# Moving three steps of ScalarE's queue ahead of the first two evictions of a tile, in gated attention with feed-forward on 8 cores

## The chip, the cores and the metric

The kernel runs on one Trainium2 chip, on all 8 of its cores (two dies of four). Each core takes one of 8 sequences of 4096 tokens and talks to no other core. The time is the device time in microseconds of the slowest core.

## What is computed

A layer of gated attention with a residual and a layer norm, and then a feed-forward network with a residual and a layer norm. Cut to what matters here:

```python
normed = (x - mu) * rsqrt(var + 1e-05) * norm_g + norm_b
hv = silu(normed @ W_h + b_h)              # 1024 -> 4096
v, gate = hv[..., :2048], hv[..., 2048:]
qk = silu(normed @ W_qk + b_qk)            # 1024 -> 128
quad_q, lin_q, quad_k, lin_k = four scaled and shifted copies of qk
attn = square(relu(quad_q @ quad_k.T / 256 + rel_bias))   # in groups of 256 tokens
lin_kv = lin_k.T @ v / n                   # over the whole sequence
out = (gate * (attn @ v + lin_q @ lin_kv)) @ W_o + b_o + x
x = layernorm(x + out)
x = layernorm(x + relu(x @ W1 + b1) @ W2 + b2)
```

## The kernel before

Everything is written out by hand, one queue of instructions per engine, with semaphores between them. `NT` is 32: the 4096 tokens of a core are 32 tiles of 128. There are three phases. Phase 1 makes v, gate and the four heads of each tile, writes them to HBM and adds up lin_kv. Phase 2 does the attention, W_o and the first layer norm. Phase 3 is the feed-forward network. Phase 2 begins only when phase 1 has ended, since it needs the whole lin_kv. Only phase 1 is touched by the change.

PSUM is held as two tensors of four banks: E0 and E1. In phase 1 banks 0 and 1 of E0 take the 512-wide outputs of the big product in turn, banks 2 and 3 of E0 take the transposed tile, and E1 takes qk (its first 128 columns), the transposed lin_k and the product for lin_kv.

PE's order in tile t (`emit_tensor`, from L653) is: `p1_T(t+1)` (L592, L598: eight 128-wide transposes of the next tile's normed input), `p1_hv(t,0)` and `p1_hv(t,1)` (a bias matmul on L623 and eight 512-wide matmuls on L626 each), `p1_qk(t+1)` (L610: eight 128-wide matmuls that read the next tile's `nfm`), `p1_hv(t,2)`, `p1_hv(t,3)`, `p1_linkT(t)` (L635), `p1_hv(t,4)`, `p1_hv(t,5)`, `p1_linkv(t)` (L645), `p1_hv(t,6)`, `p1_hv(t,7)`. Slices s = 0 to 3 are v, 4 to 7 are gate. An even slice waits until both slices of the pair ahead of it have been evicted, since a pair takes both banks:

```python
if s % 2 == 0:
    wge(tn, "c_hvev", 8 * t + s)       # L619
```

`p1_qk(u)` waits for both halves of `nfm` of tile u (`c_Tev`, L607) and for DVE's addition of lin_kv of tile u-2 (L608).

ScalarE (ACT) evicts and, for each tile, runs these helpers in the order of the loop from L887. `p1_hvev(t,s)` is a Silu from PSUM into `vt` (L865) or `gt` (L872). `p1_ev(t+1)` is two copies of the transposed next tile from PSUM into `nfm` (L845, L847). `p1_n0(t+2)` normalizes the tile after that (L835). `stats_sq(t+8)` is a square with a sum (L821), and in every fourth tile (t = 3, 7, ... 23, six in all) `sqrt_batch` follows it, a square root that waits for six small DVE instructions and needs another function table (L827). `p1_qkev(t+1)` is the Silu of qk into `qkf` (L854). It waits for p1_qk(t+1) on PE (`c_qk`) and for DVE's heads of tile t-1.

DVE, in tile t, takes the sums of tile t+8, then makes the four heads from `qkf` (L1150 to L1157), copies lin_k (L1161) and adds to lin_kv (L1167). SyncE loads x ten tiles ahead and stores v. ACT's own queue stores the gate (`g_sp`), and GpSimd stores the heads and casts W1 and W2 to bf16 in HBM, two pieces a tile.

Of the kernel before, what the change touches and what calls it, by code (L numbers as in the profile page):

```python
# [61 lines left out]
def build_program(NT=32, dbg=False, phases=3):  # L62
# [223 lines left out]
    def wge(eng, nm, v):  # L286
        if v > 0:
            eng.wait_ge(S[nm], v)
# [520 lines left out]
    def emit_scalar(sc):  # L809
# [8 lines left out]
        def stats_sq(u):  # L818
            D["x1"].wait(sc, u)
            wge(sc, "c_sqst", u - 1)  # L820
            sc.activation(T["sqscr"][:, (u % 2) * DM:(u % 2 + 1) * DM],  # L821
                          T["xt"][:, (u % XB) * DM:(u % XB + 1) * DM],
                          AF.Square, accum_out=T["sumsq"][:, u:u + 1]).then_inc(S["c_sqst"], 1)

        def sqrt_batch(g):
            wge(sc, "c_v1", g + 1)
            sc.activation(T["s_all"][:, 4 * g:4 * g + 4], T["rcp"][:, 4 * g:4 * g + 4],  # L827
                          AF.Sqrt).then_inc(S["c_sq1"], 1)

        def p1_n0(u):  # L830
            if not (0 <= u < NT):
                return
            wge(sc, "c_sv", u // 4 + 1)
            wge(sc, "c_T", 2 * u - 4)
            sc.activation(T["n0"][:, (u % 3) * DM:(u % 3 + 1) * DM],  # L835
                          T["xt"][:, (u % XB) * DM:(u % XB + 1) * DM],
                          AF.Identity, bias=T["nms"][:, u:u + 1],
                          scale=T["s_all"][:, u:u + 1]).then_inc(S["c_n0"], 1)

        def p1_ev(u):  # L840
            if not (0 <= u < NT):
                return
            wge(sc, "c_T", 2 * u + 1)
            wge(sc, "c_hvmm", 8 * u - 8)
            sc.copy(T["nfm"][:, (u % 2) * DM:(u % 2) * DM + 512], E0[:, 1024:1536]).then_inc(S["c_Tev"], 1)  # L845
            wge(sc, "c_T", 2 * u + 2)
            sc.copy(T["nfm"][:, (u % 2) * DM + 512:(u % 2) * DM + 1024], E0[:, 1536:2048]).then_inc(S["c_Tev"], 1)  # L847

        def p1_qkev(u):
            if not (0 <= u < NT):  # L850
                return
            wge(sc, "c_qk", u + 1)
            wge(sc, "c_heads", u - 1)
            sc.activation(T["qkf"][:, (u % 2) * QKD:(u % 2 + 1) * QKD],  # L854
                          E1[:, 0:QKD], AF.Silu,
                          bias=T["bqk_eff"][:]).then_inc(S["c_qkev"], 1)

        def p1_hvev(t, s):
            wge(sc, "c_hvmm", 8 * t + s + 1)
            src_ = E0[:, (s % 2) * 512:(s % 2) * 512 + 512]  # L860
            if s < 4:
                if s == 0:
                    D["vout"].wait(sc, t - 2)
                    wge(sc, "c_lkvmm", t - 1)
                sc.activation(T["vt"][:, (t % 2) * HID + s * 512:(t % 2) * HID + (s + 1) * 512],  # L865
                              src_, AF.Silu).then_inc(S["c_hvev"], 1)
            else:
                h = (s - 4) // 2
                if s in (4, 6):
                    D["gout"].wait(sc, 2 * (t - 2) + h)  # L870
                gslot = ((t % 2) * 2 + h) * DM
                sc.activation(T["gt"][:, gslot + (s % 2) * 512:gslot + (s % 2) * 512 + 512],  # L872
                              src_, AF.Silu).then_inc(S["c_hvev"], 1)
                if s in (5, 7):
                    wge(sc, "c_hvev", 8 * t + s + 1)
                    D["gout"].issue(sc, g_sp[t * 128:(t + 1) * 128, h * DM:(h + 1) * DM],
                                    T["gt"][:, gslot:gslot + DM])
# [7 lines left out]
        p1_ev(0)  # L885
        p1_qkev(0)
        for t in range(NT):  # L887
            p1_hvev(t, 0)
            p1_hvev(t, 1)
            p1_ev(t + 1)  # L890
            p1_n0(t + 2)
            u = t + L
            if u < NT:
                stats_sq(u)
                if u % 4 == 3:
                    sqrt_batch(u // 4)
            p1_hvev(t, 2)
            p1_hvev(t, 3)
            p1_qkev(t + 1)
            p1_hvev(t, 4)  # L900
            p1_hvev(t, 5)
            p1_hvev(t, 6)
            p1_hvev(t, 7)
# [87 lines left out]
        for Ti in range(NS):  # L991
# [7 lines left out]
            for tt in range(4):  # L999
                t = 4 * Ti + tt  # L1000
# [265 lines left out]
    with nc.Block() as block:  # L1266
        @block.vector
        def _(ve):
            emit_vector(ve)

        @block.sync
        def _(sync):
            emit_sync(sync)

        @block.gpsimd
        def _(gp):
            emit_gpsimd(gp)

        @block.tensor
        def _(tn):  # L1280
            emit_tensor(tn)

        @block.scalar
        def _(sc):
            emit_scalar(sc)
# [35 lines left out]
```

## Time and profile before

| | us |
|---|---|
| median of 3 runs | 2492.0 |
| lowest and highest | 2488.97, 2530.39 |
| the profiled execution | 2487.91 |
| its longest span, core 3 | 2486.4 |
| its shortest span, core 5 | 2467.1 |
| core 3: PE busy, weight loads busy | 2031.6, 860.0 |
| core 3: DVE, ACT, GpSimd busy | 541.4, 729.5, 96.7 |

A span runs from the first to the last instruction of a core. PE is TensorE's matmuls, PEld its weight loads, which lie beside them. A row of the timeline merges instructions of one kind; its bracket tells how long the engine stood idle before it and what ended the idle time. Ends of matmuls are modelled, so a PE row overlaps the next by a little. PEclk is the clock that TensorE was granted, as a share of its full 2.4 GHz.

### The profile page before, as it was taken

To read this page: it belongs to the slowest core of one execution; us is meant where nothing else is said; L and a number is where in the kernel's file an instruction comes from. 1 tells how busy PE (TensorE), PEld (TensorE's weight loads), DVE (VectorE), ACT (ScalarE), POOL (GpSimd) and SP (SyncE) were. 2 spreads that over 40 slices of the span, in tenths; PEclk is the share of its full clock that TensorE was granted. 3 is DMA by queue.
4 is the path that set the end of the run, shared out by engine and by line. 5 is a ranking of instruction groups with operands and counts; after the bars stand their busy time and mean duration, and the time that the engine had idled before them with its cause. 6 is when DMAs were issued, how large, how long until landed. Compare 5 with 4: busy or idle time off the path is not lost.

```text
span 2486.4 us, 27942 instructions; the slowest of 8 cores (2467.1 to 2486.4 us)
## 1 busy us (share of the span) xinstructions
PE 2031.6 (82%) x9498; PEld 860.0 (35%) x9498; DVE 541.4 (22%) x1127; ACT 729.5 (29%) x1192; POOL 96.7 (4%) x177
## 2 busy tenths in 40 slices
PE   0348888888888864888888858989898989898988
PEld 0113333333333321333333423434343434343433
DVE  0331221212211112444444420202020202020202
ACT  0034333333332311333333323132323232323231
POOL 1001101100111000000000000000000000000000
PEclk9869999999999987999999979999999999999999
DMA  9454433443433248766656634202020102020101
GB/s 142 69 141 102 128 114 97 133 114 105 115 90 102 87 119 247 200 195 186 192 190 193 191 89 142 74 15 72 16 70 18 67 13 73 14 78 11 51 17 51
DMA packets 125173, 256.28 MB, mean 103 GB/s; under 512 B 57614, under 2 KB 66119, under 8 KB 122985
## 3 DMA queue, kind: packets, MB, share of 16 engines
q1 hardware_dynamic: 80794, 129.42, 16.6%
q10 hardware_dynamic: 27648, 92.29, 11.5%
q0 software_dynamic: 16592, 32.78, 8.5%
q8 instruction: 80, 1.31, 0.2%
q14 instruction: 59, 0.48, 0.1%
HBM read 188.64 MB, written 112.20 MB: 121 GB/s over the span
## 4 chain that ended last, share of the span: by engine, by line
PE 72%; ACT 7%; DVE 6%; issue 6%; DMA 3%; another core or an unknown queue 3%; SPq 1%; DVEq 1%; ACTq 0%
PE E L626 19%; PE E L787 18%; PE E L770 16%; PE E L738 10%; PE E L623 3%; ACT h L996 2%; DVE sums L1218 1%; PE E L645 1%; PE E L717 1%; DMA xt<-x 1%; PE E L733 1%; DMA w<-w1bf_sp 1%; ACT vt L865 1%; DVE pre L1214 1%
## 5 line engine op out<-in xcount | busy, mean ns | idle before, releaser
L626 PE MATMUL E<-wh,nfm 128*128 128x512 bf16 x2048 | 524.0, 402 | 0.0
L770 PE MATMUL E<-xfm,w 128*128 128x512 bf16 x2048 | 457.1, 382 | 73.6 <-ACT h L996 59.4
L787 PE MATMUL E<-w,h 128*128 128x512 bf16 x2048 | 453.2, 379 | 0.0
L770 PEld LDWEIGHTS E<-xfm,w 128*128 128x128 bf16 x2048 | 197.5, 98 | 331.8 <-issue 106.1
L626 PEld LDWEIGHTS E<-wh,nfm 128*128 128x128 bf16 x2048 | 187.1, 102 | 265.8 <-issue 100.7
L787 PEld LDWEIGHTS E<-w,h 128*128 128x128 bf16 x2048 | 195.1, 98 | 241.2 <-issue 14.6
L996 ACT ACTIVATE h<-E,b_fm 128x512 bf16<-128x512 f32 x256 | 173.5, 686 | 315.4 <-PE E L770 315.4
L738 PE MATMUL E<-wo,gfm 128*128 128x512 bf16 x1024 | 253.8, 405 | 0.0
L1251 DVE TENSOR_TENSOR pre<-E,x2r 128x1024 f32<-128x1024 f32 x32 | 39.2, 1225 | 860.8 <-PE E L787 860.8
L872 ACT ACTIVATE gt<-E 128x512 f32<-128x512 f32 x128 | 76.5, 597 | 248.1 <-PE E L626 245.4
L738 PEld LDWEIGHTS E<-wo,gfm 128*128 128x128 bf16 x1024 | 100.3, 103 | 139.3 <-issue 46.0
L865 ACT ACTIVATE vt<-E 128x512 bf16<-128x512 f32 x128 | 75.8, 597 | 233.5 <-PE E L626 220.7
L1003 ACT ACTIVATE sq<-pre 128x1024 bf16<-128x1024 f32 x32 | 33.8, 1057 | 367.9 <-DVE pre L1251 367.9
L623 PE MATMUL E<-bh_eff_bf,ones 1*128 1x512 bf16 x256 | 101.1, 395 | 42.2 <-ACT vt L865 29.3
L1167 DVE TENSOR_TENSOR linkv<-linkv,E 128x2048 f32<-128x2048 f32 x31 | 70.9, 2288 | 180.5 <-PE E L645 180.5
L717 PE MATMUL E<-ident,gtm 128*128 128x128 bf16 x512 | 46.9, 228 | 74.0 <-ACT gfm L936 62.0
L699 PE MATMUL E<-v,attnT 128*128 128x512 bf16 x256 | 78.8, 390 | 31.6 <-DMA v<-v_sp 30.1
L944 ACT ACTIVATE sq<-pre 128x1024 bf16<-128x1024 f32 x32 | 33.8, 1057 | 206.5 <-DVE pre L1214 182.1
L1161 DVE CAST lktm<-E 128x128 bf16<-128x128 f32 x32 | 9.3, 292 | 351.2 <-PE E L635 351.2
L1197 DVE TENSOR_TENSOR gtm<-E,g 128x512 bf16<-128x512 f32 x128 | 79.3, 681 | 8.4 <-DMA g<-g_sp 8.4
L936 ACT CAST gfm<-E 128x512 bf16<-128x512 f32 x128 | 69.4, 585 | 8.7 <-PE E L717 5.0
L623 PEld LDWEIGHTS E<-bh_eff_bf,ones 1*128 1x128 bf16 x256 | 23.4, 91 | 137.2 <-issue 134.0
(110 smaller groups left out, 1150.5 us busy)
## 6 DMA issues: line engine op xcount, KB each, us to landing
g_sp<-gt ACTq DMA_DIRECT2D x64, 512.0 KB, 3.6
g<-g_sp ACTq DMA_DIRECT2D x64, 512.0 KB, 6.1
xt<-x SPq DMA_DIRECT2D x32, 512.0 KB, 4.5
v_sp<-vt SPq DMA_DIRECT2D x32, 512.0 KB, 2.9
v<-v_sp SPq DMA_DIRECT2D x32, 512.0 KB, 5.6
x2t<-x SPq DMA_DIRECT2D x32, 512.0 KB, 4.2
x_sp<-x2f ACTq DMA_DIRECT2D x32, 512.0 KB, 5.7
x2r<-x_sp SPq DMA_DIRECT2D x32, 512.0 KB, 4.2
```

The costliest lines, as they stand in the source:

```text
L623: tn.matmul(pslc, T["ones1"][:], T["bh_eff_bf"][0:1, s * 512:(s + 1) * 512], start=True, stop=False)
L626: mm = tn.matmul(pslc, T["nfm"][:, sl2 + c * 128:sl2 + (c + 1) * 128], T["wh"][:, c * 2 * HID + s * 512:c * 2 * HID + (s + 1) * 512], star ...
L699: tn.matmul(ps, T["attnT"][:, a0:a0 + 128], T["v2"][:, (vtile % 3) * HID + b * 512:(vtile % 3) * HID + (b + 1) * 512], start=(j == 0), sto ...
L717: mm = tn.matmul(E0[:, bank + k * 128:bank + (k + 1) * 128], T["gtm"][:, (u % 2) * HID + ch * 128:(u % 2) * HID + (ch + 1) * 128], ID, sta ...
L738: mm = tn.matmul(ps, T["gfm"][:, (u % 2) * HID + k * 128:(u % 2) * HID + (k + 1) * 128], T["wo"][:, k * DM + h * 512:k * DM + (h + 1) * 51 ...
L770: mm = tn.matmul(ps, T["w1"][:, dc * 4096 + ci * 128:dc * 4096 + (ci + 1) * 128], T["xfm3"][:, (Ti % 2) * 4 * DM + dc * 512:(Ti % 2) * 4 * ...
L787: mm = tn.matmul(ps, T["h1"][:, ci * 512 + tt * 128:ci * 512 + (tt + 1) * 128], T["w2"][:, ci * DM + h * 512:ci * DM + (h + 1) * 512], sta ...
L865: sc.activation(T["vt"][:, (t % 2) * HID + s * 512:(t % 2) * HID + (s + 1) * 512], src_, AF.Silu).then_inc(S["c_hvev"], 1)
L872: sc.activation(T["gt"][:, gslot + (s % 2) * 512:gslot + (s % 2) * 512 + 512], src_, AF.Silu).then_inc(S["c_hvev"], 1)
L996: sc.activation(T["h1"][:, ci * 512:(ci + 1) * 512], E0[:, (ci % 4) * 512:(ci % 4 + 1) * 512], AF.Relu, bias=T["b1_fm"][:, ci:ci + 1]).the ...
L1167: ve.tensor_tensor(T["linkv"][:], T["linkv"][:], E1[:, :], ALU.add).then_inc(S["c_lkvadd"], 1)
L1197: ve.tensor_tensor(T["gtm"][:, (tau % 2) * HID + b * 512:(tau % 2) * HID + (b + 1) * 512], E1[:, b * 512:(b + 1) * 512], T["g2"][:, gsl:gs ...
```

## The change

In ACT's loop over tiles, the eviction of the next tile's transposes, the normalization of the tile after it and the eviction of the next tile's qk now stand ahead of the evictions of slices 0 and 1, in the order ev, n0, qkev. The queues of the other engines and all waits inside the helpers stay as they are.

```diff
--- before.py
+++ after.py
@@ -885,10 +885,11 @@
         p1_ev(0)
         p1_qkev(0)
         for t in range(NT):
+            p1_ev(t + 1)
+            p1_n0(t + 2)
+            p1_qkev(t + 1)
             p1_hvev(t, 0)
             p1_hvev(t, 1)
-            p1_ev(t + 1)
-            p1_n0(t + 2)
             u = t + L
             if u < NT:
                 stats_sq(u)
@@ -896,7 +897,6 @@
                     sqrt_batch(u // 4)
             p1_hvev(t, 2)
             p1_hvev(t, 3)
-            p1_qkev(t + 1)
             p1_hvev(t, 4)
             p1_hvev(t, 5)
             p1_hvev(t, 6)
```

## Rows read from the trace of the kernel before

**Rows 1.** The page of the slowest core: chain that ended last, shares by engine.
```profile
PE 72%; ACT 7%; DVE 6%; issue 6%; DMA 3%; another core or an unknown queue 3%; SPq 1%; DVEq 1%; ACTq 0%
```

**Rows 2.** Stage 157.5 to 918 us of core 3: busy by engine, PEclk, DMA share, GB/s.
```profile
157.50:918.00 760.50, 657.49 (x2952) 256.31 (x2951) 152.61 (x258) 266.27 (x447) 85.42 (x160) 0.94 0.39 107
```

**Rows 3.** Waits of PE in that stage: us in total, times, longest us.
```profile
PE E L610 <- ACT nfm L847: 59.3, 31, 1.9
```

**Rows 4.** PE timeline, one tile: start us, us, line, [idle before <-releaser].
```profile
403.79 0.61 PE L610 MATMUL E<-nfm,wqk 128*128 128x128 bf16 x8 [1.92 <-ACT nfm L847]
404.33 0.48 PE L623 MATMUL E<-bh_eff_bf,ones 1*128 1x512 bf16 x1
404.75 3.44 PE L626 MATMUL E<-wh,nfm 128*128 128x512 bf16 x8
...
408.44 1.90 PE L626 MATMUL E<-wh,nfm 128*128 128x512 bf16 x8
410.18 0.22 PE L635 MATMUL E<-ident,lkfm 128*128 128x128 bf16 x1
411.18 0.37 PE L623 MATMUL E<-bh_eff_bf,ones 1*128 1x512 bf16 x1 [0.78 <-ACT vt L865]
...
421.57 0.37 PE L623 MATMUL E<-bh_eff_bf,ones 1*128 1x512 bf16 x1 [0.39 <-ACT gt L872]
```

**Rows 5.** ACT timeline of the same tile.
```profile
402.94 0.60 ACT L847 CAST nfm<-E 128x512 bf16<-128x512 f32 x1
403.41 1.26 ACT L835 ACTIVATE n<-xt,nms,s_all 128x1024 bf16<-128x1024 f32 x1
404.56 1.06 ACT L821 ACTIVATE sqscr<-xt 128x1024 bf16<-128x1024 f32 x1
...
410.44 0.60 ACT L865 ACTIVATE vt<-E 128x512 bf16<-128x512 f32 x1 [1.55 <-PE E L626]
410.93 0.36 ACT L854 ACTIVATE qkf<-E,bqk_eff 128x128 f32<-128x128 f32 x1
```

**Rows 6.** Granted clock (third value from the right) in 404.6 to 407.9 us.
```profile
404.60:407.90 3.30, 3.30 (x9) 1.05 (x8) 0.00 (x0) 1.11 (x3) 0.00 (x0) 0.50 0.41 84
```

**Rows 7.** PE timeline, starts of L610 in three later tiles of core 3.
```profile
427.84 0.61 PE L610 MATMUL E<-nfm,wqk 128*128 128x128 bf16 x8 [1.92 <-ACT nfm L847]
...
452.31 0.61 PE L610 MATMUL E<-nfm,wqk 128*128 128x128 bf16 x8 [1.92 <-ACT nfm L847]
...
453.16 1.90 PE L626 MATMUL E<-wh,nfm 128*128 128x512 bf16 x8
...
474.71 0.61 PE L610 MATMUL E<-nfm,wqk 128*128 128x128 bf16 x8 [1.92 <-ACT nfm L847]
```

**Rows 8.** ACT timeline of the tile at 426 us, which loads two tables.
```profile
431.61 1.28 ACT L827 ACT_TABLE_LOAD   x1 [1.85 <-DVE rcp L1117]
...
434.42 1.08 ACT L865 ACTIVATE vt<-E 128x512 bf16<-128x512 f32 x2
```

**Rows 9.** PE timeline of two tiles with table loads, core 3, then core 1.
```profile
722.73 0.37 PE L623 MATMUL E<-bh_eff_bf,ones 1*128 1x512 bf16 x1 [1.58 <-ACT vt L865]
...
332.60 0.58 PE L623 MATMUL E<-bh_eff_bf,ones 1*128 1x512 bf16 x1 [2.28 <-ACT vt L865]
333.12 3.59 PE L626 MATMUL E<-wh,nfm 128*128 128x512 bf16 x8
```

**Rows 10.** PE timeline of core 3, the first of the tiles.
```profile
163.98 0.61 PE L610 MATMUL E<-nfm,wqk 128*128 128x128 bf16 x8 [1.80 <-ACT nfm L847]
```

**Rows 11.** Lines L626 and L770 on core 1, then the same on core 3.
```profile
L626 PE MATMUL E<-wh,nfm x2048: 379/379/634, 155.2 to 907.1; 128*128 128x512 bf16 x187
...
L770 PE MATMUL E<-xfm,w x2048: 376/379/634, 1468.5 to 2401.9; 128*128 128x512 bf16 x187
...
L626 PE MATMUL E<-wh,nfm x2048: 379/379/634, 157.6 to 916.1; 128*128 128x512 bf16 x187
...
L770 PE MATMUL E<-xfm,w x2048: 376/379/634, 1483.7 to 2416.7; 128*128 128x512 bf16 x187
```

## What the change should do to the time

> **What bounds the kernel now.** I read the chain that ended last first, and PE holds 72% of it [rows 1]. So an edit counts if it shortens PE's stalls, or makes its matmuls faster, in the stage where it is made. That stage is phase 1, from 157.5 to 918 us on core 3 [rows 2]. PE is busy there for 657.5 of 760.5 us, its clock is 0.94, and ACT is busy for only 266.3 us and DVE for 152.6 us. No engine other than PE is full, and the DMA share is 0.39. The other engines matter through the moments at which PE waits for them. In PE's waits the largest stands at L610, p1_qk(t+1), for ACT's second copy into nfm: 59.3 us in 31 waits [rows 3].
>
> One tile shows why. The pair of slices 0 and 1 ends at 401.87 (403.79 less the idle 1.92), and then p1_qk waits 1.92 us [rows 4]. ACT has to evict slice 1 first, because it stands ahead of the two copies in its queue, though the transposes that these copies read ended some 4 us before. The reader is to see a second cost in the same rows: the eight matmuls of L626 after the stall took 3.44 us, those after them 1.90 us. The clock was 0.50, the 1.2 GHz level, from 404.6 to 407.9 us [rows 6], after PE had stood idle for 1.92 us. It is not so in every tile: after the stall that ended at 452.31 the eight took 1.90 us [rows 7]. So from one L610 to the next a plain tile takes 24.05 us with such a fall (403.79 to 427.84) and 22.40 us without (452.31 to 474.71). A fall costs 1.65 us [rows 4, 7]. On core 3 the clock fell after 25 of the 31 stalls, the first of them at 163.98 after only 1.80 us [rows 10]; on the other cores after 14 to 26.
>
> **The change, part by part.** Nothing is added or removed. It moves five ACT instructions: two copies, the normalization and the Silu of qk ahead of Silus of slices 0 and 1. ACT issues no DMA in between, and SP's and POOL's queues are not touched. SP's load of x waits for the normalization, which now comes earlier, but the store of v that stands behind evictions 0 to 3 in SP's order still sets its pace, so nothing starts much sooner.
>
> *The copies and the normalization.* They now follow the last gate eviction and its store, and need the transposes, which are over before slice 0 starts at 421.57 [rows 4]. Two copies of at most 0.60 and the normalization, pitch 1.15 (403.41 to 404.56) [rows 5], are 2.4 us. They lie beside slices 0 and 1, which take 4.35 us (421.57 to 425.92, which is 427.84 less 1.92) [rows 4, 7]. Cost nothing, with near 2 us of cover. So p1_qk no longer waits: a stall of 1.92 us goes.
>
> *What is late next.* The Silu of qk is a new wait in front of the evictions of slices 0 and 1, which before ran under slice 1 and under the stall. Slice 2 needs both banks free, so PE waits behind p1_qk instead, for three ACT instructions. After the pair ends, p1_qk ends 0.45 us later: it starts 0.16 before the modelled end, as L635 does (408.44 + 1.90 = 410.34, L635 at 410.18), and its row is 0.61 long [rows 4]. ACT starts 0.10 later, as at 410.44 after 410.34. Then comes the Silu of qk, 0.36 long [rows 5]. No row shows an eviction directly behind it. Neighbours on ACT overlap by 0.11: 0.60 long and 0.49 apart, 1.26 long and 1.15 apart [rows 5]. I take 0.25; without overlap it would be 0.36, and below 0.25 nothing points. The two evictions are 0.49 and 0.60, and PE starts 0.14 after them (410.44 + 0.60 to 411.18) [rows 4, 5]. So the new stall is 0.10 + 0.25 + 0.49 + 0.60 + 0.14 = 1.58 us (up to 1.69), and slice 2 starts 0.45 + 1.58 = 2.03 us after the pair's end. Before, it was 404.33 less 401.87, 2.46 us [rows 4]. A tile gains 0.43 us (0.32 to 0.43).
>
> The Trainium skill, "ScalarE: Activation LUTs", section "What ACT_TABLE_LOAD costs", says that back-to-back ACTIVATEs overlap by about 93 ns. By that the pitch would be 0.27 and the stall 1.60 us, the sum hardly other.
>
> *The clock.* This is the larger term. After stalls between 1.06 and 1.62 us no fall follows anywhere in phase 1, on any core, some 30 in all; one is the 1.58 at 722.73 [rows 9]. After 1.80 it fell [rows 10], after 1.92 mostly. The new stall is nearest to 722.73, so I take no fall in a plain tile. The bounds are none and all 31. What speaks against it is that small matmuls (p1_qk) now stand ahead of the stall and not behind.
>
> *Tiles with table loads.* In six tiles the square is followed by DVE's small instructions (a wait of 1.85), a table load, the root, and a second load, before the evictions of slices 2 and 3 at 434.42 [rows 8]. This chain, not PE, sets when slice 4 starts, with or without a fall at slice 2. It begins with the square, 2.69 us after the pair's end (404.56 less 401.87) [rows 4, 5]. In the new order that is 0.45 + 0.10 + 0.25 + 0.49 + 0.49 = 1.78, so slice 4 starts 0.91 us earlier. PE reaches it earlier too: slice 3 ends 2.03 + 4.35 = 6.38 after the pair, and slice 4 starts at 434.42 + 1.08 + 0.14 less 425.92 less 0.91, 8.81. The stall there is some 2.4 us. The nearest row is core 1's 2.28, behind which L626 took 3.59 [rows 9]. Over the eight cores ten of sixteen such stalls were followed by a fall. I take three of six at 1.65 each, 5.0 us. The bounds are none and six falls that reach over both slices, 6 x 3.3 = 19.8 us.
>
> *Downstream.* From the last L626 to the first L770 core 3 took 567.6 us, while core 1, which was 9 us ahead, took 561.4 [rows 11]. Until now the cores came out of phase 1 apart, since they had different numbers of falls; with none they come out together and load W1 together. I leave core 3's own 567.6 and add 3 us for the slowest of eight with different luck in the table tiles; the bounds are 0 and 6.
>
> **The sum**, on core 3, the slowest, against the profiled 2487.9 us: 25 plain tiles x 0.43 = 10.8. Nineteen of these had a fall, 19 x 1.65 = 31.4. Six table tiles x 0.91 = 5.5. Together 47.7. Less 5.0 and less 3 leaves 39.7 us, so 2448 us. The median of the runs before, 2492.0, is 4 us above the profiled one, and the lowest is 2489.0; I take the lower end and stay at 2448.
>
> **Rivals.**
>
> *1. The forecast*: no falls in plain tiles, about half in table tiles. 2448 us, its own range 2441 to 2458. Chance 0.57.
>
> *2. Falls almost gone from phase 1.* The new stalls in table tiles mostly miss, or the cores' loads at the start of phase 2 collide less. Without the 5.0 and the 3 it is 2487.9 - 47.7 = 2440, and with core 1's passage (6 us less) 2434. The only thing for it is that six of sixteen such stalls were not followed by a fall [rows 9]. Chance 0.17.
>
> *3. The fall moves with the stall.* 1.58 to 1.69 us lies just under the 1.80 that was followed by one [rows 10]. If 19 plain tiles still have it, only 10.8 + 5.5 - 5.0 = 11.3 us remain: 2477 us. Against it speaks the 1.58 of core 3 [rows 9]. Chance 0.17. The Trainium skill, "TensorE: Matmul & The Clock Gate", section "A second HAM failure mode: psum-queue depth-cycling", says that short idles between groups of matmuls as banks are cycled are enough to make the clock oscillate. By that rule the new stall would do what the old one did. The trace shows it for the 1.92 us stall and does not for those of 0.78 us.
>
> *4. The other side: a fall after each of the 31 new stalls, and a double one in each table tile.* Core 3 had 25 falls. In plain tiles there would be six more, 6 x 1.65 = 9.9 against the 10.8 gained. In table tiles 19.8 are lost against 5.5. That gives 2487.9 - 10.8 + 9.9 - 5.5 + 19.8 = 2501 us. It turns slower than before once falls in phase 1 cost more than 16.3 us above those of before, ten more than now. It needs all 31 stalls to be hit, where the longer ones of today are missed 6 times in 31. Chance 0.06.
>
> *5. A plain delay on ACT*, such as extra table loads from the new order, 2 x 1.28 us a tile [rows 8], 79 us over 31 tiles. Today the Silu of slice 3 is followed by the Silu of qk and copies by the normalization with no load between [rows 5], and the order brings no new pair of functions but those. Chance 0.03.
>
> **How the numbers follow.** The likeliest is 2448 us. From 2436 to 2478 lie rivals 1 and 3 and most of 2, a bit over 8 in 10. A measurement of this kernel can tell about 2% from no change. Faster by over 2% is under 2438 us: half of rival 2 and a tail of the forecast, 0.18. Slower by over 2% is over 2538 us: rival 5, 0.03. Within 2%: 0.79.
>
> **What would show it.** L610 has no idle time behind nfm any more. The idle time stands at L623 of slice 2, released by ACT's vt, 1.6 us in 25 plain tiles. L626 of slice 2 is 1.90 long and not 3.3 to 3.4; a plain tile takes 21.97 us. Slice 4 of a table tile waits 2.4 us. PEclk of phase 1 rises from 0.94 to 0.98 or more, and the stage is some 43 us shorter, while phases 2 and 3 keep their length. It would be wrong if slice 2 shows over 1.75 us of idle time, if L626 behind it still takes 3.4, or if copies or normalization outlast slice 1.

## The result: 0.7% faster, where 1.6% was forecast

| | before | after |
|---|---|---|
| median of 10 runs | 2490.1 us | 2474.3 us |
| lowest | 2487.5 us | 2465.9 us |
| the profiled execution | 2487.9 us | 2465.9 us |
| its longest span | 2486.4 us (core 3) | 2464.4 us (core 5) |

The ratio of after to before is 0.9928, with a 95% interval from 0.9915 to 0.9941. In some executions the cores of one die run at a lower clock; the ratio leaves these out. By this ratio the kernel is faster beyond doubt, by 18 us, and by less than 2%. The forecast was 2448 us, 40 us faster. The measured 2474.3 lies inside the range, 2436 to 2478, but where rival 3 put it (2477) and not where the likeliest case did.

The stalls moved as the prediction had it. These are PE's waits in phase 1 of core 5, the slowest (us in total, times, longest us):

```profile
PE E L623 <- ACT vt L865: 81.9, 64, 2.3
PE E L623 <- ACT gt L872: 12.8, 32, 0.8
```

The wait at L610 for nfm [rows 3] is gone. In its place L623 waits for vt 64 times and not 33.

In PE's timeline three tiles of core 5 follow each other here (start, us, line, idle before):

```profile
433.92 0.61 PE L610 MATMUL E<-nfm,wqk 128*128 128x128 bf16 x8
436.17 0.37 PE L623 MATMUL E<-bh_eff_bf,ones 1*128 1x512 bf16 x1 [1.64 <-ACT vt L865]
436.47 1.90 PE L626 MATMUL E<-wh,nfm 128*128 128x512 bf16 x8
...
455.93 0.61 PE L610 MATMUL E<-nfm,wqk 128*128 128x128 bf16 x8
458.18 0.37 PE L623 MATMUL E<-bh_eff_bf,ones 1*128 1x512 bf16 x1 [1.64 <-ACT vt L865]
458.48 3.27 PE L626 MATMUL E<-wh,nfm 128*128 128x512 bf16 x8
...
479.54 0.61 PE L610 MATMUL E<-nfm,wqk 128*128 128x128 bf16 x8
```

p1_qk starts with no idle time, and slice 2 then waits 1.64 us. From one L610 to the next it is 22.01 us from 433.92 (forecast 21.97) and 23.61 us from 455.93. In the first of these tiles L626 behind the stall is 1.90 long, in the second 3.27. The stall is 1.64 us in both. The granted clock (third value from the right) behind the first stall and behind the second is:

```profile
436.50:438.40 1.90, 1.90 (x10) 0.76 (x9) 0.00 (x0) 0.56 (x2) 0.00 (x0) 1.00 1.44 164
459.00:462.20 3.20, 3.20 (x8) 0.84 (x6) 0.00 (x0) 0.43 (x2) 0.00 (x0) 0.50 0.90 108
```

ACT's timeline of another tile:

```profile
385.05 0.59 ACT L847 CAST nfm<-E 128x512 bf16<-128x512 f32 x1
385.52 1.25 ACT L835 ACTIVATE n<-xt,nms,s_all 128x1024 bf16<-128x1024 f32 x1
389.05 0.37 ACT L854 ACTIVATE qkf<-E,bqk_eff 128x128 f32<-128x128 f32 x1 [2.28 <-PE E L610]
389.32 1.07 ACT L865 ACTIVATE vt<-E 128x512 bf16<-128x512 f32 x2
390.27 1.07 ACT L821 ACTIVATE sqscr<-xt 128x1024 bf16<-128x1024 f32 x1
```

The copies and the normalization are over at 386.8, well ahead of the Silu of qk at 389.05. That Silu and the next eviction start 0.27 apart, where the estimate was 0.25. Of a tile with table loads:

```profile
416.85 0.22 PE L635 MATMUL E<-ident,lkfm 128*128 128x128 bf16 x1
419.34 0.37 PE L623 MATMUL E<-bh_eff_bf,ones 1*128 1x512 bf16 x1 [2.27 <-ACT vt L865]
419.64 1.90 PE L626 MATMUL E<-wh,nfm 128*128 128x512 bf16 x8
```

Slice 4 waits 2.27 us, where 2.4 was forecast. And the whole of phase 1 on core 5 (busy us by engine, then the granted clock, the DMA share and GB/s):

```profile
core 5: us, PE busy (x) PEld busy (x) DVE busy (x) ACT busy (x) POOL busy (x), PEclk, DMA share, GB/s
151.00:887.00 736.00, 640.86 (x2952) 255.11 (x2951) 152.59 (x258) 266.12 (x447) 85.41 (x160) 0.96 0.47 110
```

It is 735 us long where core 3 took 759 before. Its clock is 0.96, against 0.94 [rows 2] and the 0.98 or more that the forecast wanted to see. Over the eight cores the clock fell after 116 of 240 stalls of 1.58 to 1.64 us, nearly all of them 1.64 (13 to 16 of 30 on each core). Before the change it fell after 149 of 240 stalls of 1.92 us.

### The profile page after: what moved, and what is told of

Read it like the earlier page. It is cut to its first block, busy times and chain, and to the rows that moved or that the text cites. A ratio compares the mean times of both kernels' runs of the same rounds, so it can differ in the third digit from the quotient of the medians.

```text
span 2464.4 us, 27942 instructions; the slowest of 8 cores (2452.0 to 2464.4 us)
## 1 busy us (share of the span) xinstructions
PE 2019.7 (82%) x9498; PEld 860.5 (35%) x9498; DVE 541.4 (22%) x1127; ACT 728.8 (30%) x1192; POOL 96.7 (4%) x177
## 4 chain that ended last, share of the span: by engine, by line
PE 73%; ACT 7%; DVE 6%; issue 6%; DMA 3%; another core or an unknown queue 3%; SPq 1%; DVEq 1%; ACTq 0%
PE E L626 19%; PE E L787 18%; PE E L770 17%; PE E L738 10%; PE E L623 3%; ACT h L996 2%; ACT vt L865 2%; DVE sums L1218 1%; PE E L645 1%; PE E L717 1%; DMA xt<-x 1%; DMA w<-w1bf_sp 1%; PE E L733 1%; DVE pre L1214 1%
## 5 line engine op out<-in xcount | busy, mean ns | idle before, releaser
L770 PE MATMUL E<-xfm,w 128*128 128x512 bf16 x2048 | 461.5, 384 | 74.9 <-ACT h L996 59.3
L626 PE MATMUL E<-wh,nfm 128*128 128x512 bf16 x2048 | 510.4, 394 | 0.0
L770 PEld LDWEIGHTS E<-xfm,w 128*128 128x128 bf16 x2048 | 198.6, 99 | 336.5 <-issue 113.5
L626 PEld LDWEIGHTS E<-wh,nfm 128*128 128x128 bf16 x2048 | 183.8, 100 | 256.9 <-issue 85.3
L623 PE MATMUL E<-bh_eff_bf,ones 1*128 1x512 bf16 x256 | 100.4, 392 | 94.7 <-ACT vt L865 81.9
L623 PEld LDWEIGHTS E<-bh_eff_bf,ones 1*128 1x128 bf16 x256 | 23.4, 91 | 189.2 <-issue 189.2
```

Of the source, the lines that this page charges most:

```text
L623: tn.matmul(pslc, T["ones1"][:], T["bh_eff_bf"][0:1, s * 512:(s + 1) * 512], start=True, stop=False)
L626: mm = tn.matmul(pslc, T["nfm"][:, sl2 + c * 128:sl2 + (c + 1) * 128], T["wh"][:, c * 2 * HID + s * 512:c * 2 * HID + (s + 1) * 512], star ...
L770: mm = tn.matmul(ps, T["w1"][:, dc * 4096 + ci * 128:dc * 4096 + (ci + 1) * 128], T["xfm3"][:, (Ti % 2) * 4 * DM + dc * 512:(Ti % 2) * 4 * ...
```

## The experiments

Two theories of these falls were put against each other. **A**: the eight 128-wide matmuls of p1_qk, which stand directly at the stall, are part of what brings the clock down. **B**: a stall of 1.64 us does it by its length alone, whatever stands beside it, and the quiet stalls of this length before the change [rows 9] were a few lucky ones. A third, **C**, sought the lost gain at the start of phase 2.

The falls below are counted from the clock records of all eight cores, for the stalls of one kind in phase 1. A stall counts as followed by a fall when a stretch at the lower clock begins during it or within about 2 us of its end.

### e2_small_away and e3_small_ahead: the same stall, with and without small matmuls directly ahead

Both lengthen the stall in the same way, by scratch copies on ACT ahead of eviction 1. Both have p1_qkev behind eviction 3 again. Only e2 moves p1_qk on PE.

```diff
@@ e2_small_away, against the changed kernel @@
 (PE)
             p1_hv(t, 0)
-            p1_hv(t, 1)
             p1_qk(t + 1)
+            p1_hv(t, 1)
             p1_hv(t, 2)
 (ACT)
             p1_ev(t + 1)
             p1_n0(t + 2)
-            p1_qkev(t + 1)
             p1_hvev(t, 0)
+            p1_dummy(t)
             p1_hvev(t, 1)
...
             p1_hvev(t, 3)
+            p1_qkev(t + 1)
@@ the new helper on ACT @@
+            wge(sc, "c_hvmm", 8 * t + 2)
+            for w in (256, 256):
+                wge(sc, "c_dmy", ndmy[0])
+                sc.copy(T["dmy"][:, 0:w], E0[:, 512:512 + w]).then_inc(S["c_dmy"], 1)
+                ndmy[0] += 1
@@ e3_small_ahead: the same on ACT with (256, 256, 256), PE as in the changed kernel @@
```

> As e1, but PE runs p1_qk(t+1) between slices 0 and 1, so that a full slice stands ahead of the stall, and ACT makes two copies of 256 columns of bank 1 into a scratch tile ahead of eviction 1, which stretch the stall at slice 2 to about 1.64 us. Tile length 22.0 us without a fall, as in the changed kernel. Theory A: no falls in plain tiles, phase 1 of about 714 us and a time near 2448. Theory B: falls after about half of the stalls, phase 1 of 735 and a time near 2472, as in the changed kernel.

> The control of e2: the same scratch copies on ACT, three of them, but p1_qk(t+1) stays directly ahead of the stall, which is again about 1.64 us. Both theories: falls after about half of the stalls and a time near 2472. If it had no falls, neither the small matmuls nor the stall's length would be the cause, but something in the order of ACT's work.

e2 took 2463.1 us, ratio 0.9882 (0.9858 to 0.9905). e3 took 2480.2 us, ratio 0.9941 (0.9912 to 0.9969). PE's timeline of one tile of e2 (p1_qk is L611 here, the slices L624 and L627), and under it all of phase 1 on the same core, with columns as above:

```profile
389.39 0.61 PE L611 MATMUL E<-nfm,wqk 128*128 128x128 bf16 x8
389.94 0.38 PE L624 MATMUL E<-bh_eff_bf,ones 1*128 1x512 bf16 x1
390.25 1.90 PE L627 MATMUL E<-wh,nfm 128*128 128x512 bf16 x8
393.78 0.37 PE L624 MATMUL E<-bh_eff_bf,ones 1*128 1x512 bf16 x1 [1.62 <-ACT vt L866]
394.08 1.90 PE L627 MATMUL E<-wh,nfm 128*128 128x512 bf16 x8
...
161.00:880.00 719.00, 621.95 (x2952) 251.99 (x2951) 152.51 (x258) 285.91 (x508) 85.36 (x160) 0.99 0.39 113
```

PE's timeline of e3, the stall of a tile with a fall and of the next without, and then phase 1:

```profile
380.90 0.37 PE L624 MATMUL E<-bh_eff_bf,ones 1*128 1x512 bf16 x1 [1.64 <-ACT vt L866]
381.20 2.67 PE L627 MATMUL E<-wh,nfm 128*128 128x512 bf16 x8
...
402.26 0.61 PE L611 MATMUL E<-nfm,wqk 128*128 128x128 bf16 x8
404.51 0.37 PE L624 MATMUL E<-bh_eff_bf,ones 1*128 1x512 bf16 x1 [1.64 <-ACT vt L866]
404.81 1.90 PE L627 MATMUL E<-wh,nfm 128*128 128x512 bf16 x8
...
163.00:900.00 737.00, 642.43 (x2952) 255.50 (x2951) 152.52 (x258) 297.75 (x539) 85.46 (x160) 0.96 0.40 110
```

The stalls are 1.62 and 1.64 us. In e2 a full slice stands ahead of the stall and p1_qk one slice earlier, in e3 p1_qk stands directly ahead. In e2 the clock fell after none of 230 stalls of 1.62 us or a little less, nor after ten of 1.84. Each core also had one of 1.90 us, and after four of these eight it fell. In e3 it fell after 109 of 240, much like the changed kernel. A plain tile without a fall is 22.0 us in both. e2's granted clock in phase 1 is 0.99, e3's 0.96, and phase 1 is 719 us against 737. This is theory A, and against B: the same idle time, in a tile of the same length, brings the clock down only with the small matmuls directly ahead of it. So the changed kernel's falls come from what the change put next to the stall.

The time of e2 was 15 us above its expectation. 5 us of this lie in phase 1, where 29 of 48 table tiles took 25.2 us or more. The rest is behind phase 1: on its slowest core 577 us from the end of the slices to phase 3's first matmul (L770 before, L771 here), where core 3 took 567 before [rows 11], and 1007.4 us from there to the end, where core 3 took 1002.7. e3 was 8 us above its expectation.

### e8_longer_stall: how much do the small matmuls count?

```diff
@@ against e2_small_away @@
-            for w in (256, 256):
+            for w in (256, 256, 256):
```

> The kernel of e2 with one more scratch copy on ACT ahead of eviction 1: the stall at slice 2, with a full slice ahead of it and behind it, grows from 1.62 to 2.08 us, which is e3's stall of 1.63 plus the 0.45 us that the small matmuls took there. If the small matmuls count for the clock as almost nothing, falls follow after about as many stalls as in e3 (109 of 240). If they count for about half, after clearly more. If a long stall between full slices never brings the clock down, after none. Tile of 22.46 us without a fall; with falls after half of them a time near 2490, without near 2478.

```profile
405.80 1.90 PE L627 MATMUL E<-wh,nfm 128*128 128x512 bf16 x8
409.79 0.45 PE L624 MATMUL E<-bh_eff_bf,ones 1*128 1x512 bf16 x1 [2.08 <-ACT vt L866]
410.17 3.46 PE L627 MATMUL E<-wh,nfm 128*128 128x512 bf16 x8
```

One run took 2506.5 us beside 2495.3 for the kernel before, where 2490 was expected with falls after half of the stalls. The stall is 2.08 us between full slices, and the clock fell after 192 of 222 of them, behind this one too (L627, 3.46). So idle time alone is enough when it is long, and 0.46 us more of it did more than the small matmuls do in e3: they are not the same as idle time. How much less they are is not settled by this run, since the tile is 0.45 us longer too, and e5 shows that the share of falls hangs on more than the stall and its neighbours.

### e1_ev_first: only the copies and the normalization go ahead

```diff
@@ against the changed kernel @@
             p1_ev(t + 1)
             p1_n0(t + 2)
-            p1_qkev(t + 1)
             p1_hvev(t, 0)
...
             p1_hvev(t, 3)
+            p1_qkev(t + 1)
             p1_hvev(t, 4)
```

> Only the two copies and the normalization go ahead of evictions 0 and 1; the Silu of qk stays behind eviction 3. Theory A (the clock falls because the eight small matmuls of L610 stand directly at the stall and count for little): slice 2 waits 0.10 + 0.60 + 0.14 less 0.45 = 0.4 us for eviction 1, and no fall follows in a plain tile. Theory B (the length of the stall alone decides, and 1.64 us is enough): the same, since 0.4 us is short. Both expect a plain tile of 22.40 - 2.46 + 0.85 = 20.8 us (22.0 in the changed kernel), table tiles of 22.4, and about 2410 us against 2488 before. Theory C (the gain is lost again where phase 2 begins, because the cores come out together): a passage from the last L626 to the first L770 longer than 570 us and a time over 2420.

```profile
401.71 0.61 PE L610 MATMUL E<-nfm,wqk 128*128 128x128 bf16 x8
402.71 0.37 PE L623 MATMUL E<-bh_eff_bf,ones 1*128 1x512 bf16 x1 [0.39 <-ACT vt L865]
403.02 1.90 PE L626 MATMUL E<-wh,nfm 128*128 128x512 bf16 x8
...
162.00:841.00 679.00, 618.65 (x2951) 251.47 (x2951) 152.57 (x258) 265.72 (x446) 85.36 (x160) 0.99 0.42 120
```

It took 2419.4 us, ratio 0.9721 (0.9629 to 0.9813), 9 us above its expectation. Slice 2 waits 0.39 us and no fall follows, on any core. A plain tile is 20.77 us. Only in table tiles, whose slice 4 still waits 2.27 us, the clock fell, in 17 of 48. So two of the three steps moved are worth some 50 us more than all three (ratios 0.9721 and 0.9928): the third, the Silu of qk ahead of evictions 0 and 1, costs 1.25 us of stall in each tile and all the falls of plain tiles. Theory C finds something, but little. The passage to phase 3 took 563 to 572 us on the eight cores, before 558 to 567, and three of them passed the 570 us that the theory wanted.

### e4: each slice waits for its own bank

```diff
@@ against e1_ev_first @@
-            if s % 2 == 0:
-                wge(tn, "c_hvev", 8 * t + s)
+            wge(tn, "c_hvev", 8 * t + s - 1)
```

> As e1, and each slice waits for the eviction of its own bank alone (slice s for eviction s-1 and not for both of the pair ahead). The stalls at slices 0, 2 and 4 go (0.39, 0.4 and 0.78 us). Plain tile 19.25 us, no falls; table tiles keep a stall of some 2.35 us at slice 4 and take 21.6 us. 25 x 3.15 + 31 + 6 x 2.9 - 5 = 122 us less than before: about 2366 us. If something other than PE becomes the bound (ACT's chain, the load of x), a plain tile is longer than 19.6 us.

> The kernel of e4 again, for a profile of all eight cores at the granted clock of the other runs. Cores 0 to 3 of e4 took 623 us for phase 1 and 2342 to 2354 us in all; so 2358 us, with no falls in plain tiles, and a plain tile of 19.25 us.

The first gave a ratio of 0.9477 (0.943 to 0.9525). The second took 2359.0 us, ratio 0.9463 (0.9436 to 0.9489), 7 us under the first expectation and 1 us above the second. PE's timeline of the second:

```profile
387.22 0.37 PE L622 MATMUL E<-bh_eff_bf,ones 1*128 1x512 bf16 x1 [1.79 <-ACT vt L864]
...
401.32 0.61 PE L610 MATMUL E<-nfm,wqk 128*128 128x128 bf16 x8
401.86 0.38 PE L622 MATMUL E<-bh_eff_bf,ones 1*128 1x512 bf16 x1
402.18 1.90 PE L625 MATMUL E<-wh,nfm 128*128 128x512 bf16 x8
...
406.07 0.22 PE L634 MATMUL E<-ident,lkfm 128*128 128x128 bf16 x1
406.22 0.39 PE L622 MATMUL E<-bh_eff_bf,ones 1*128 1x512 bf16 x1
```

No slice of a plain tile waits for anything any more, behind p1_qk at 401.32 neither. A plain tile takes 19.01 us, a table tile 21.4 without a fall. This version beats both kernels, by 5.4% and 4.7%.

### e5_own_bank_only and e6_after_own_bank: the own-bank wait with the two other orders

```diff
@@ e5: the kernel before, and e6: the changed kernel @@
-            if s % 2 == 0:
-                wge(tn, "c_hvev", 8 * t + s)
+            wge(tn, "c_hvev", 8 * t + s - 1)
```

> The order of evictions of the kernel before, and each slice waits for the eviction of its own bank alone. The stalls of 0.39 and 0.78 us go, that of 1.92 us at p1_qk stays, since it waits for the copies and these stand behind eviction 1. Theory A: the small matmuls still follow that stall at once, so falls stay as frequent as before (14 to 26 a core); a plain tile takes 21.2 us without and 22.9 with a fall, and the time is 31 x 1.17 = 36 us less than before, about 2453. If the own-bank wait were all that matters, it would be near e4's 2358.

> The changed kernel with own-bank waits. Slice 2 now waits for the Silu of qk and for eviction 0, not for eviction 1: a stall of 0.10 + 0.25 + 0.60 + 0.14 = 1.1 us directly behind the small matmuls. Theory A: at 1.1 us the small matmuls do not bring the clock down (in the changed kernel they did at 1.64), so no falls and a plain tile of 20.35 us, 34 us above e4: about 2392. If the clock still falls after half of them, some 25 us more, 2417.

e5 took 2438.3 us, ratio 0.9819 (0.9742 to 0.9896), e6 2404.3 us, ratio 0.9654 (0.9623 to 0.9684). PE's timelines, e5 and then e6:

```profile
405.24 0.61 PE L610 MATMUL E<-nfm,wqk 128*128 128x128 bf16 x8 [1.92 <-ACT nfm L846]
...
406.10 2.86 PE L625 MATMUL E<-wh,nfm 128*128 128x512 bf16 x8
```

```profile
391.21 0.61 PE L610 MATMUL E<-nfm,wqk 128*128 128x128 bf16 x8
392.98 0.37 PE L622 MATMUL E<-bh_eff_bf,ones 1*128 1x512 bf16 x1 [1.15 <-ACT vt L864]
393.28 1.90 PE L625 MATMUL E<-wh,nfm 128*128 128x512 bf16 x8
...
399.77 0.37 PE L622 MATMUL E<-bh_eff_bf,ones 1*128 1x512 bf16 x1 [1.79 <-ACT vt L864]
400.07 3.31 PE L625 MATMUL E<-wh,nfm 128*128 128x512 bf16 x8
```

In e5 the stall of 1.92 us with the small matmuls behind it stays, and with it the falls. But they were fewer than expected: 83 after 240 stalls of 1.9 to 2.0 us, where the kernel before had 149 of 240. The stall and what directly adjoins it are the same. The tile is 1.3 us shorter (21.09 us without a fall, before 22.40), and the short stalls at slices 0 and 4 are gone. So how often a stall brings the clock down depends on more than its length and its neighbours; whether it is the spacing of the stalls or the missing short ones no run separates. This is a miss of 15 us in its expectation.

In e6 the stall behind the small matmuls is 1.09 to 1.16 us and no fall followed any of 240, nor any of eight of 1.37: with small matmuls beside it too, the stalls that were followed by a fall were longer. It was 12 us slower than expected. The rows at 399.77 and 400.07 show most of it: in table tiles slice 4's stall of 1.79 us brought the clock down in 40 of 48 cases, five a core and so some 8 us, in the second run of e4 in 11 of 48. Why so much more often is open.

### e7_qk_late_on_pe: the other way to make the copies early enough

```diff
@@ against the kernel before, PE @@
             p1_hv(t, 1)
-            p1_qk(t + 1)
             p1_hv(t, 2)
             p1_hv(t, 3)
             p1_linkT(t)
+            p1_qk(t + 1)
```

> ACT's order as before; on PE p1_qk(t+1) moves behind slice 3 and the transpose of lin_k, so that the copies are ready when PE reaches it. Stalls: slice 2 waits 0.10 + 0.60 + 0.14 = 0.85 us for eviction 1, slice 4 waits 0.78 - 0.45 = 0.33. The sum of stalls in a tile is that of e1, 1.57 us, in other places: plain tile 20.8 us, no falls, table tiles 22.4 to 22.9, a time of 2410 to 2425, equal to e1. If the order of ACT's queue has an effect of its own beyond these stalls, it differs from e1 by more than 10 us.

```profile
385.40 0.37 PE L623 MATMUL E<-bh_eff_bf,ones 1*128 1x512 bf16 x1 [0.84 <-ACT vt L865]
...
389.65 0.61 PE L610 MATMUL E<-nfm,wqk 128*128 128x128 bf16 x8
390.60 0.37 PE L623 MATMUL E<-bh_eff_bf,ones 1*128 1x512 bf16 x1 [0.34 <-ACT vt L865]
...
406.18 0.37 PE L623 MATMUL E<-bh_eff_bf,ones 1*128 1x512 bf16 x1 [0.84 <-ACT vt L865]
```

Its fastest run took 2431.8 us, one number without an interval. That is 7 us above the expected range and 12 us above e1, more than the 10 us that the expectation had named. Slice 2 waits 0.84 us and slice 4, at 390.60, 0.34; from 385.40 to 406.18 it is 20.78 us, e1's tile to 0.01. So the order of ACT's queue has no effect of its own on a plain tile; the stalls are all. The 12 us lie in and around the table tiles. These are worse than e1's, 23.6 to 25.0 us, since p1_qk now stands behind p1_linkT, which there waits for DVE's heads. The tile ahead of each takes 23.2 to 23.5, and the clock fell at each of the 48.

## Why the prediction was wrong

**What bounds the kernel, and the stall that goes**: right. The copies and the normalization lie beside slices 0 and 1, and L610 waits no more.

**What is late next**: right. The new stall is 1.64 us (forecast 1.58, at most 1.69), the tile 22.01 us (21.97), so a plain tile without a fall gains 0.39 us and not 0.43. The overlap of neighbours on ACT holds for the Silu of qk too, 0.10 where 0.11 was taken. The figure of the Trainium skill, "ScalarE: Activation LUTs", "What ACT_TABLE_LOAD costs", was the nearer one: it gave 1.60 us.

**The price of a fall**: right, 1.60 us a tile (23.61 less 22.01), where 1.65 was taken.

**The clock in plain tiles**: this step failed. "I take no fall in a plain tile" rested on some 30 stalls of 1.06 to 1.62 us that no fall had followed [rows 9]. The traces have 40 of them, but only six of 1.56 to 1.62. All 40 stood between full slices, with only the one small matmul of L635 beside them, and the six came at most 2.6 us after a stretch at the lower clock. The one at 722.73 had this slow slice ahead of it:

```profile
715.63 3.31 PE L626 MATMUL E<-wh,nfm 128*128 128x512 bf16 x8
```

The new stall has eight small matmuls directly ahead, and past the first tile no such stretch just before it. The text named the small matmuls as what spoke against it and then gave them no weight. e2 and e3 show that it decides: none of 230, and 109 of 240, both without such a stretch past the first tile. Core 5 had 12 falls in its 25 plain tiles, 12 x 1.60 = 19.2 us, against a sum of zero. The sum had counted 31.4 us for falls that go; on core 5 only 31.4 - 19.2 = 12.2 us came.

**Table tiles**: near. The forecast was 6 x 23.56 + 5.0 = 146.4 us for the six of a core, and core 5 took 143.9. The falls came elsewhere than forecast, three at slice 2, where they cost such a tile next to nothing, and one at slice 4.

**Downstream**: right in size for the passage, 571.1 us on core 5 (from 886.2 to 1457.3) against 570.6 in the sum. Two things outside the sum nearly cancelled, which was luck: core 5 began its first slice at 151.3 us, 6 us ahead of core 3 before, and took 1007.1 us from the first L770 to the end against 1002.7. So the 19.2 us of falls account for the 18 us by which the profiled execution (2465.9 us) missed. The median lies 8 us higher; no trace shows what those executions took more. In e2 the two did not cancel, and even there, with no falls in plain tiles, the time was 2463 and not 2448: 3 us was too little for the stages behind phase 1. The prediction had phase 3 keep its length, and the spread there goes with the clock as well. In the ten profiles of both kernels, e1 to e3, e4's second run and e5 to e8 (80 cores), it took 1002.5 to 1003.2 us on the 35 cores with three stretches at the lower clock in it, and 1006.6 to 1008.1 us on the 28 with five, core 5 among them.

**The rivals**: rival 3, 0.17, is what happened. That its price (2477) is within 3 us of the median is in part luck: it took 19 falls in plain tiles, and the profiled execution had 10 to 13 on each core and took 2465.9 us. Its argument was a poor one too: that 1.6 lies close under 1.80. The length alone did not do it. The rule of the Trainium skill that stood there ("TensorE: Matmul & The Clock Gate", "A second HAM failure mode: psum-queue depth-cycling"), that short idles between groups of matmuls are enough to make the clock oscillate, pointed the right way. The runs narrow it: idles of 0.78 to 1.62 us between full slices did nothing, those of 1.64 behind small matmuls did it in half of the cases. Rivals 1, 2, 4 and 5 did not occur.

## What to carry to other kernels

When a change moves a stall, look at what adjoins the new one, and at what came shortly before the old ones, before reading its price from stalls of the same length: here it was small matmuls that turned a harmless 1.6 us into a halved clock in half of the tiles. A step hoisted on an in-order queue helps only if what it waits for is early too; the copies and the normalization passed this, the Silu of qk did not, and taken alone the first two gained 70 us where all three gained 18. And a wait for a pair of banks where the work needs one may cost more than any order of the queue: here a wait for each slice's own bank gained 60 us more.

## What the runs showed of the hardware

- The granted clock fell to its lower level (1.2 GHz) after 0 of 230 stalls of 1.62 us between full slices, after 109 of 240 of 1.63 us with eight 128-wide matmuls directly ahead, and after 192 of 222 of 2.08 us between full slices. Of the few in between it fell after none of ten of 1.84 us and four of eight of 1.90, between full slices too. With L635's one small matmul ahead, 1.79 us did it in 11 of 48 cases in e4's second run and in 40 of 48 in e6.
- It fell after none of 240 stalls of 1.09 to 1.16 us with the same small matmuls ahead.
- With a stall of 1.92 us and the same matmuls on both sides of it, it fell in 149 of 240 tiles of 22.4 us (counted without a fall) and in 83 of 240 (stalls of 1.9 to 2.0) of 21.1 us. What sets this share was not settled.
- Phase 3 took 1002.5 to 1003.2 us on cores with three stretches at the lower clock in it, 1004.7 to 1006.1 with four, and 1006.6 to 1008.1 with five.
- An ACTIVATE of 128 columns from PSUM, 0.37 us long, is followed by the next after 0.27 us.
